# An eight-batch role adapter with layer norm: stores move to GpSimd's queue, loads are issued a batch earlier, VectorE's steps are put in another order

## The chip, the cores and the metric

The kernel runs on one core of one Trainium2 chip. The metric is the device time of one execution in microseconds. TensorE does the matrix products, VectorE and ScalarE work on the elements, GpSimd computes one small quantity per tile of rows, and SyncE issues the loads (and, before the change, the stores).

## The reference

For each of 8 batches `x` is 512 rows of 1024 columns, and a role (1 or 2, drawn per batch) picks the weights.

```python
h = einsum('bsh,bhk->bsk', x, W_down[role]) + b_down[role]     # 1024 -> 512
h = gelu(h, approximate=False)
u = einsum('bsk,bkh->bsh', h, W_up[role]) + b_up[role]         # 512 -> 1024
y = x + u
yn = (y - mean(y)) * rsqrt(var(y) + 1e-05)                     # over the 1024 columns
return yn * gamma[role] + beta[role]
```

Everything is float32.

## The kernel before, in words

**Precision by three passes.** Each float32 operand is held as a rounded part (`_hi`, made by a ScalarE copy) and a rest (`_lo`, made by a VectorE subtraction, called a split below). A product is the sum of three matmuls: hi by hi, hi by lo, lo by hi. `x` and `W_down` come in four parts of 128 x 1024 per batch (`x_stage`, `wd_stage`, 512 KB each), `W_up` in four (`wu_stage`), the residual rows in four tiles of 128 x 1024 (`rows`), and there is one buffer of each. Three rows (`b_up_row`, `gamma_row`, `beta_row`) are spread to 128 partitions for each batch.

**TensorE** (L256 to L307). A batch is a down phase and an up phase of 96 matmuls each (128x512). The down phase walks parts 0 and 1 first (48 matmuls), and then makes the four column blocks kc = 0 to 3 of `down_ps` final one after the other, 12 matmuls each. The up phase makes four row tiles t = 0 to 3 in two `up_ps` buffers, 24 matmuls each; in tile 0 the six matmuls of block kc wait for `h_split` of that block (L305). Tiles 2 and 3 of `up_ps` wait until VectorE has summed tiles 0 and 1 (L295).

**ScalarE** (L376 to L396) makes `x_hi`, `wd_hi`, `wu_hi`, applies gelu to each kc (`h_full`, L346) and rounds it (`h_hi`, L348), and computes mean and sum of squares of a row tile (L353 to L356).

**VectorE** (L519 to L556) splits `wu`, `x`, `wd` and `h`, adds `b_up` to the rows when they have landed (`bias_tile`, L479), adds `up_ps` to them with a row sum (`sum_tile`, L484), centres and scales by gamma (`centre_tile`, L501, which writes into the memory of `h_full`), and finishes with 1/deviation and beta (`finish_tile`, L515). **GpSimd** makes 1/deviation of each tile (L425, L427), in order of the tiles.

**SyncE** (L187 to L212) issues all loads and stores of a batch in one fixed order, and stands at each wait until it is met. `rows` of the next batch can be loaded into tile t only when the store of tile t has landed (L177). The order of every engine's work is the order in which the code is written.

Of the kernel before, what the change touches and what calls it, by code (L numbers as in the profile page):

```python
# [5 lines left out]
P = 128  # L6
# [10 lines left out]
def bass_role_adapter_layernorm(  # L17
# [17 lines left out]
    NLOAD = 4  # L35
# [6 lines left out]
    with ExitStack() as ctx:  # L42
# [110 lines left out]
        def _(sp):  # L153
# [29 lines left out]
            def store(b, t):  # L183
                sp.wait_ge(normed, NT * b + t + 1)
                sp.dma_start(out[b, t * P:(t + 1) * P, :], rows[:, t, :]).then_inc(stored[t], 16)
# [37 lines left out]
            for i in range(KC):  # L223
                load_wu_part(first_role, i)
            steps(0)
            with sp.Fori(1, B - 1) as b:
                steps(b)
            steps(B - 1)
            for i in range(HALVES):
# [3 lines left out]
            for t in range(NT - 1):  # L233
                sp.wait_ge(stored[t], 16 * B)
            sp.wait_ge(stored[NT - 1], 16 * (B - 1))
            sp.wait_ge(last_stored, 16 * HALVES)
# [81 lines left out]
        def _(act):  # L318
# [8 lines left out]
            def round_next_part(b, i):  # L327
# [283 lines left out]
```

## Time and profile before

| | us |
|---|---|
| three runs | 377.04, 380.54, 381.19 (median 380.54) |
| profiled execution, its own time | 377.03 |
| its span, first to last instruction | 374.9 |
| TensorE busy | 355.9 (95%) |
| VectorE busy | 288.3 (77%) |
| ScalarE busy | 184.0 (49%) |
| GpSimd busy | 41.1 (11%) |
| mean granted TensorE clock | 0.994 |

The profiled execution's own time is 2.1 us over its span, and it is at the lower end of the runs shown. Busy time counts a matmul from its start to its modelled end (390 ns), though the next one starts after 227 ns, so the waits of TensorE are read from the starts of its matmuls rather than from its share of busy time.

### The profile page before, as it was taken

To read this page: it belongs to the slowest core of one execution; us is meant where nothing else is said; L and a number is where in the kernel's file an instruction comes from. 1 tells how busy PE (TensorE), PEld (TensorE's weight loads), DVE (VectorE), ACT (ScalarE), POOL (GpSimd) and SP (SyncE) were. 2 spreads that over 40 slices of the span, in tenths; PEclk is the share of its full clock that TensorE was granted. 3 is DMA by queue.
4 is the path that set the end of the run, shared out by engine and by line. 5 is a ranking of instruction groups with operands and counts; after the bars stand their busy time and mean duration, and the time that the engine had idled before them with its cause. 6 is when DMAs were issued, how large, how long until landed. Compare 5 with 4: busy or idle time off the path is not lost.

```text
span 374.9 us, 4895 instructions
## 1 busy us (share of the span) xinstructions
PE 355.9 (95%) x1548; PEld 289.0 (77%) x1548; DVE 288.3 (77%) x293; ACT 184.0 (49%) x297; POOL 41.1 (11%) x71
## 2 busy tenths in 40 slices
PE   7999899969999999999999999999999999999991
PEld 3888678848888788877888788887888878888881
DVE  2797888598875987859877788859887598793475
ACT  4793635655156643377263753546515664335132
POOL 0000120001200041001210013000120004100011
PEclk9999999999999999999999999999999999999997
DMA  7999925996189932999249972699618994391022
GB/s 210 377 408 409 386 118 180 410 368 276 64 260 409 413 142 112 324 384 405 83 147 381 372 311 112 201 382 407 242 62 267 378 412 168 140 326 40 0 112 112
DMA packets 27081, 96.58 MB, mean 258 GB/s; under 512 B 3138, under 2 KB 3138, under 8 KB 27074
## 3 DMA queue, kind: packets, MB, share of 16 engines
q1 hardware_dynamic: 26928, 96.48, 68.1%
q8 instruction: 4, 0.07, 0.1%
q10 hardware_dynamic: 146, 0.01, 0.0%
q14 instruction: 3, 0.02, 0.0%
HBM read 79.70 MB, written 16.78 MB: 257 GB/s over the span
## 4 chain that ended last, share of the span: by engine, by line
DMA 25%; DVE 22%; PE 17%; issue 14%; POOL 9%; ACT 5%; SPq 5%; ACTq 1%; DVEq 1%; POOLq 0%
DMA out<-rows 12%; PE up_ps L251 11%; DVE rows L484 8%; DMA rows<-x 8%; POOL rstd L427 6%; PE down_ps L244 6%; DMA x_stage<-xT 5%; DVE x_lo L456 4%; DVE wd_lo L461 3%; DVE rows L515 3%; DVE h_lo L472 3%; ACT squares L356 3%; POOL var_eps L425 2%; ACT neg_mean_scaled L353 1%; SPq L178 1%
## 5 line engine op out<-in xcount | busy, mean ns | idle before, releaser
L251 PE MATMUL up_ps<-wu_hi,h_hi 128*128 128x512 f32 x256 | 80.3, 392 | 9.0 <-DVE h_lo L472 7.2
L244 PE MATMUL down_ps<-x_hi,wd_hi 128*128 128x512 f32 x256 | 81.8, 390 | 1.0 <-ACT wd_hi L407 0.9
L244 PE MATMUL down_ps<-x_lo,wd_hi 128*128 128x512 f32 x256 | 81.4, 389 | 0.0
L244 PE MATMUL down_ps<-x_hi,wd_lo 128*128 128x512 f32 x256 | 81.4, 389 | 0.0
L251 PE MATMUL up_ps<-wu_lo,h_hi 128*128 128x512 f32 x256 | 79.6, 389 | 0.0
L251 PE MATMUL up_ps<-wu_hi,h_lo 128*128 128x512 f32 x256 | 79.5, 389 | 0.0
L251 PEld LDWEIGHTS up_ps<-wu_hi,h_hi 128*128 128x128 f32 x256 | 47.4, 188 | 21.9 <-issue 9.9
L479 DVE TENSOR_TENSOR rows<-rows,b_up_row 128x1024 f32<-128x1024 f32 x32 | 38.7, 1224 | 30.8 <-DMA rows<-x 30.7
L515 DVE SCALAR_TENSOR_TENSOR rows<-h_full,rstd,beta_row 128x1024 f32<-128x1024 f32 (+1 forms) x33 | 41.2, 1252 | 22.7 <-POOL rstd L427 21.4
L353 ACT ACTIVATE neg_mean_scaled<-row_sum 128x1 f32<-128x1 f32 x31 | 6.3, 203 | 106.2 <-DVE rows L484 106.2
L244 PEld LDWEIGHTS down_ps<-x_hi,wd_hi 128*128 128x128 f32 x256 | 47.8, 188 | 11.8 <-issue 1.9
L251 PEld LDWEIGHTS up_ps<-wu_lo,h_hi 128*128 128x128 f32 x256 | 48.1, 188 | 10.1
L251 PEld LDWEIGHTS up_ps<-wu_hi,h_lo 128*128 128x128 f32 x256 | 48.1, 188 | 10.1
L244 PEld LDWEIGHTS down_ps<-x_hi,wd_lo 128*128 128x128 f32 x256 | 48.1, 188 | 10.0
L244 PEld LDWEIGHTS down_ps<-x_lo,wd_hi 128*128 128x128 f32 x256 | 48.1, 188 | 9.9
L346 ACT ACTIVATE h_full<-down_ps,b_down_all 128x512 f32<-128x512 f32 x32 | 22.0, 686 | 59.0 <-PE down_ps L244 59.0
L501 DVE SCALAR_TENSOR_TENSOR h_full<-rows,neg_mean,gamma_row 128x1024 f32<-128x1024 f32 (+1 forms) x33 | 41.2, 1251 | 10.0 <-ACT neg_mean L354 9.4
L425 POOL TENSOR_TENSOR var_eps<-var,eps 128x1 f32<-128x1 f32 x31 | 10.1, 326 | 322.9 <-ACT squares L356 322.9
L456 DVE TENSOR_TENSOR x_lo<-x_stage,x_hi 128x1024 fp32r<-128x1024 f32 x32 | 39.0, 1219 | 7.3 <-ACT x_hi L405 3.9
L484 DVE SCALAR_TENSOR_TENSOR rows<-up_ps,rows 128x1024 f32<-128x1024 f32 x31 | 37.8, 1219 | 4.1 <-PE up_ps L251 4.1
L461 DVE TENSOR_TENSOR wd_lo<-wd_stage,wd_hi 128x1024 fp32r<-128x1024 f32 x32 | 39.0, 1219 | 2.0 <-ACT wd_hi L409 1.8
L467 DVE TENSOR_TENSOR wu_lo<-wu_stage,wu_hi 128x1024 fp32r<-128x1024 f32 x32 | 37.3, 1219 | 0.2
(37 smaller groups left out, 232.9 us busy)
## 6 DMA issues: line engine op xcount, KB each, us to landing
wu_stage<-W_up SPq DMA_DIRECT2D x32, 512.0 KB, 12.6
rows<-x SPq DMA_DIRECT2D x32, 512.0 KB, 7.2
x_stage<-xT SPq DMA_DIRECT2D x31, 512.0 KB, 8.2
wd_stage<-W_down SPq DMA_DIRECT2D x31, 512.0 KB, 9.1
out<-rows SPq DMA_DIRECT2D x31, 512.0 KB, 2.6
b_up_row<-b_up SPq DMA_DIRECT2D x8, 512.0 KB, 14.0
gamma_row<-gamma SPq DMA_DIRECT2D x8, 512.0 KB, 8.9
beta_row<-beta SPq DMA_DIRECT2D x8, 512.0 KB, 9.6
```

What stands on the lines that cost most here:

```text
L244: return pe.matmul(down_ps[:, kc, :], wd_part[:, n, c * K + kc * P:c * K + (kc + 1) * P], x_part[:, n, c * S:(c + 1) * S], start=start, st ...
L251: mm = pe.matmul(up_ps[:, t % 2, half], h_part[:, kc, t * P:(t + 1) * P], wu_part[:, kc, half], start=(kc == 0 and h_part is h_hi and wu_p ...
L346: act.activation(h_full[:, kc, :], down_ps[:, kc, :], ACT.Gelu, bias=bias).then_inc(h_full_ready, 1)
L425: pool.tensor_tensor(var_eps[:, t:t + 1], var[:, t:t + 1], eps[:, :], ALU.add).then_inc(var_eps_ready, 1)
L427: pool.tensor_tensor(rstd[:, t:t + 1], var_eps[:, t:t + 1], minus_half[:, :], ALU.pow).then_inc(rstd_ready, 1)
L456: dve.tensor_tensor(x_lo[:, i, :], x_stage[:, i, :], x_hi[:, i, :].bitcast(F32), ALU.subtract).then_inc(x_split, 1)
L461: dve.tensor_tensor(wd_lo[:, i, :], wd_stage[:, i, :], wd_hi[:, i, :].bitcast(F32), ALU.subtract).then_inc(wd_split, 1)
L467: dve.tensor_tensor(wu_lo[:, i, :], wu_stage[:, i, :], wu_hi[:, i, :].bitcast(F32), ALU.subtract).then_inc(wu_split, 1)
L479: dve.tensor_tensor(rows[:, t, :], rows[:, t, :], b_up_row[:, :], ALU.add).then_inc(biased, 1)
L484: dve.scalar_tensor_tensor(out=rows[:, t, :], in0=up_ps[:, t % 2, :], scalar=1.0, in1=rows[:, t, :], op0=ALU.mult, op1=ALU.add, accum_out= ...
L501: dve.scalar_tensor_tensor(out=centred[:, t % 2, half], in0=rows[:, t, half], scalar=neg_mean[:, t:t + 1], in1=gamma_row[:, half], op0=ALU ...
L515: dve.scalar_tensor_tensor(out=rows[:, t, half], in0=centred[:, t % 2, half], scalar=rstd[:, t:t + 1], in1=beta_row[:, half], op0=ALU.mult ...
```

## The change

The first seven batches are stored by GpSimd: after the 1/deviation of each tile it waits for that tile's `finish_tile` and issues the store from its own queue. Only the last batch is still stored by SyncE. SyncE now issues the loads of `x` and `W_down` of batch b+2 at the end of its steps for batch b, where it issued those of b+1 during batch b. VectorE puts the split of `wu` parts between the steps of the last tile of the batch before, splits part 0 of `x` and `wd` ahead of the first `h`, puts one split of the next batch's part 1 between two `h` splits, and adds the bias to tile 3 behind `h` block 2; parts 2 and 3 are split before and during tile 0's steps. ScalarE makes `x_hi` of parts 0 and 1 ahead of the first gelu, and parts 2 and 3 ahead of the first variance. TensorE's program is the same.

```diff
-            def load_next_part(b, next_role, i):
-                sp.wait_ge(x_split, NLOAD * b + i + 1)
-                load_x_part(b + 1, i)
-                sp.wait_ge(wd_split, NLOAD * b + i + 1)
-                load_wd_part(next_role, i)
+            def load_ahead(batch, role, i):
+                sp.wait_ge(x_split, NLOAD * (batch - 1) + i + 1)
+                load_x_part(batch, i)
+                sp.wait_ge(wd_split, NLOAD * (batch - 1) + i + 1)
+                load_wd_part(role, i)
...
             def steps(b):
                 first, last = is_first(b), is_last(b)
                 role = load_role(sp, b)
-                if not last:
-                    next_role = load_role(sp, b + 1)
-                    load_next_part(b, next_role, 0)
-                if first:
-                    load_role_row(b_up_row, b_up, role, b_up_landed)
                 load_rows(b, 0)
                 load_rows(b, 1)
                 if not first:
-                    store(b - 1, NT - 1)
-                load_rows(b, 2)
+                    load_rows(b, 2)
+                    sp.wait_ge(normed, NT * b)
                 load_role_row(gamma_row, gamma, role, gamma_landed)
                 load_role_row(beta_row, beta, role, beta_landed)
+                if first:
+                    load_rows(b, 2)
                 load_rows(b, 3)
-                if not last:
+                if last:
+                    return
+                next_role = load_role(sp, b + 1)
+                if first:
                     for i in range(1, NLOAD):
-                        load_next_part(b, next_role, i)
-                    for i in range(KC):
-                        sp.wait_ge(wu_split, KC * b + i + 1)
-                        load_wu_part(next_role, i)
-                    sp.wait_ge(biased, NT * (b + 1))
-                    load_role_row(b_up_row, b_up, next_role, b_up_landed)
-                for t in range(NT - 1):
-                    store(b, t)
+                        load_ahead(1, next_role, i)
+                for i in range(KC):
+                    sp.wait_ge(wu_split, KC * b + i + 1)
+                    load_wu_part(next_role, i)
+                sp.wait_ge(biased, NT * (b + 1))
+                load_role_row(b_up_row, b_up, next_role, b_up_landed)
+                if isinstance(b, int) and b + 2 == B:
+                    return
+                role_after = load_role(sp, b + 2)
+                for i in range(NLOAD):
+                    load_ahead(b + 2, role_after, i)
...
@@ ScalarE
+                act.wait_ge(up_ready, NT * b)
+                round_wu(b, 0)
+                variance(b - 1, NT - 1)
+                for i in range(1, KC):
+                    round_wu(b, i)
+                if not last:
+                    round_next_part(b, 0)
+                    round_next_x(b, 1)
                 gelu(b, 0, role)
                 if not last:
-                    round_next_part(b, 0)
+                    round_wd_part(b + 1, 1)
                 gelu(b, 1, role)
                 gelu(b, 2, role)
                 gelu(b, 3, role)
                 if not last:
-                    round_next_part(b, 1)
                     round_next_part(b, 2)
+                    round_next_part(b, 3)
                 variance(b, 0)
-                if not last:
-                    round_next_part(b, 3)
...
@@ GpSimd
+            def store(b, t):
+                pool.wait_ge(normed, NT * b + t + 1)
+                pool.dma_start(out[b, t * P:(t + 1) * P, :], rows[:, t, :]).then_inc(stored[t], 16)
...
             with pool.Fori(0, B - 1) as b:
                 for t in range(NT):
                     inverse_deviation(b, t)
+                    store(b, t)
...
@@ VectorE, the first batch
+            def first_steps():
...
+                for t in range(NT):
+                    bias_tile(0, t)
+                sum_tile(0, 0)
+                split_x_part(1, 1)
+                split_wd_part(1, 1)
+                centre_tile(0, 0)
+                finish_tile(0, 0)
+                split_x_part(1, 2)
+                sum_tile(0, 1)
...
@@ VectorE, the others
+            def down_steps(b):
+                last = is_last(b)
+                sum_tile(b - 1, NT - 1)
+                split_wu(b, 0)
+                centre_tile(b - 1, NT - 1)
+                split_wu(b, 1)
+                finish_tile(b - 1, NT - 1)
+                split_wu(b, 2)
+                split_wu(b, 3)
+                for t in range(NT - 1):
+                    bias_tile(b, t)
...
+            def steps(b):
+                down_steps(b)
+                split_x_part(b + 1, 2)
+                split_wd_part(b + 1, 2)
+                sum_tile(b, 0)
+                split_x_part(b + 1, 3)
+                centre_tile(b, 0)
+                split_wd_part(b + 1, 3)
+                finish_tile(b, 0)
+                for t in range(1, NT - 1):
+                    sum_tile(b, t)
+                    centre_tile(b, t)
+                    finish_tile(b, t)
```

The first place is VectorE in the loop over the batches, around the up phase's start: before, from the four bias tiles (L479) to the end of the `h` splits (L472).

```order
L479 TENSOR_TENSOR rows<-rows,b_up_row 128x1024 [waits rows_landed0,b_up_landed]
L479 TENSOR_TENSOR rows<-rows,b_up_row 128x1024 [waits rows_landed1]
L479 TENSOR_TENSOR rows<-rows,b_up_row 128x1024 [waits rows_landed2]
L479 TENSOR_TENSOR rows<-rows,b_up_row 128x1024 [waits rows_landed3]
L472 TENSOR_TENSOR h_lo<-h_full,h_hi 128x512 [waits h_hi_ready]
L455 ISA
L456 TENSOR_TENSOR x_lo<-x_stage,x_hi 128x1024 [waits x_hi_ready]
L461 TENSOR_TENSOR wd_lo<-wd_stage,wd_hi 128x1024 [waits wd_hi_ready]
L472 TENSOR_TENSOR h_lo<-h_full,h_hi 128x512 [waits h_hi_ready] x3
```

The same place in the changed kernel, from the third bias tile on, where L512 is the bias, L490 and L495 are the splits of `x` and `wd`, and L505 is that of `h`:

```order
L512 TENSOR_TENSOR rows<-rows,b_up_row 128x1024 [waits rows_landed2]
L489 ISA
L490 TENSOR_TENSOR x_lo<-x_stage,x_hi 128x1024 [waits x_hi_ready]
L495 TENSOR_TENSOR wd_lo<-wd_stage,wd_hi 128x1024 [waits wd_hi_ready]
L505 TENSOR_TENSOR h_lo<-h_full,h_hi 128x512 [waits h_hi_ready]
L489 REGISTER_ALU
L490 TENSOR_TENSOR x_lo<-x_stage,x_hi 128x1024 [waits x_hi_ready]
L505 TENSOR_TENSOR h_lo<-h_full,h_hi 128x512 [waits h_hi_ready]
L495 TENSOR_TENSOR wd_lo<-wd_stage,wd_hi 128x1024 [waits wd_hi_ready]
L505 TENSOR_TENSOR h_lo<-h_full,h_hi 128x512 [waits h_hi_ready]
L512 TENSOR_TENSOR rows<-rows,b_up_row 128x1024 [waits rows_landed3]
L505 TENSOR_TENSOR h_lo<-h_full,h_hi 128x512 [waits h_hi_ready]
```

Between `h` blocks 0 and 1 stood an `x` and a `wd` split; now one `x` split stands there, part 0 comes ahead of all `h` splits, and the bias of tile 3, which waits for the last rows to land, has moved from ahead of block 0 to behind block 2.

The second place is GpSimd's loop, of which one tile is shown; before:

```order
L425 TENSOR_TENSOR var_eps<-var,eps 128x1 [waits var_ready]
L427 TENSOR_TENSOR rstd<-var_eps,minus_half 128x1 [waits var_eps_ready]
L424 REGISTER_ALU
L425 TENSOR_TENSOR var_eps<-var,eps 128x1 [waits var_ready]
L427 TENSOR_TENSOR rstd<-var_eps,minus_half 128x1 [waits var_eps_ready]
```

and now, with the wait for `finish_tile` (L473) and the store between two tiles' 1/deviation:

```order
L454 TENSOR_TENSOR var_eps<-var,eps 128x1 [waits var_ready]
L456 TENSOR_TENSOR rstd<-var_eps,minus_half 128x1 [waits var_eps_ready]
L473 ISA [waits normed]
L473 DMA out<-rows 128x1024
L453 REGISTER_ALU
L454 TENSOR_TENSOR var_eps<-var,eps 128x1 [waits var_ready]
L456 TENSOR_TENSOR rstd<-var_eps,minus_half 128x1 [waits var_eps_ready]
```

The third is SyncE at the start of a batch in the loop. Before, the store of tile 3 (L185) and all waits on `stored` share its queue:

```order
L161 ISA [waits x_split]
L161 DMA x_stage<-xT 128x1024
L164 ISA [waits wd_split]
L164 DMA wd_stage<-W_down 128x1024
L177 REGISTER_ALU
L178 ISA [waits stored0]
L178 DMA rows<-x 128x1024
L178 ISA [waits stored1]
L178 DMA rows<-x 128x1024
L184 ISA
L185 ISA [waits normed]
L185 DMA out<-rows 128x1024
```

and now:

```order
L179 ISA [waits stored0]
L179 DMA rows<-x 128x1024
L179 ISA [waits stored1]
L179 DMA rows<-x 128x1024
L179 ISA [waits stored2]
L179 DMA rows<-x 128x1024
L182 ISA [waits normed]
L182 DMA gamma_row<-gamma 128x1024
L182 DMA beta_row<-beta 128x1024
L179 ISA [waits stored3]
L179 DMA rows<-x 128x1024
```

The four stores are gone from SyncE, and the loads of `x` and `W_down` that stood at its start are issued at the end of the steps of two batches earlier.

## Rows read from the trace of the kernel before

**Rows 1.** The page: the span, and each engine's busy time (share, instructions)

```profile
span 374.9 us, 4895 instructions
...
PE 355.9 (95%) x1548; PEld 289.0 (77%) x1548; DVE 288.3 (77%) x293; ACT 184.0 (49%) x297; POOL 41.1 (11%) x71
```

**Rows 2.** TensorE's waits: waiting line, releaser, us in total, times, longest

```profile
PE up_ps L251 <- DVE h_lo L472: 7.2, 7, 2.2
PE up_ps L251 <- DVE rows L484: 1.8, 2, 1.6
```

**Rows 3.** Chain of waits, in order of time: start, us, what

```profile
107.17 7.77 DMA out<-rows
115.09 4.91 DMA rows<-x
...
345.35 21.77 PE up_ps L251 x96
```

**Rows 4.** TensorE's timeline, batches 0 to 2: start, duration, work, idle before

```profile
6.84 2.41 PE L244 MATMUL down_ps<-x_hi,wd_hi 128*128 128x512 f32 x8 [0.94 <-ACT wd_hi L407]
...
39.72 0.39 PE L251 MATMUL up_ps<-wu_hi,h_lo 128*128 128x512 f32 x1
...
80.28 0.70 PE L251 MATMUL up_ps<-wu_hi,h_hi 128*128 128x512 f32 x2 [1.25 <-DVE h_lo L472]
...
123.47 0.61 PE L251 MATMUL up_ps<-wu_hi,h_lo 128*128 128x512 f32 x2
124.87 0.70 PE L251 MATMUL up_ps<-wu_hi,h_hi 128*128 128x512 f32 x2 [0.78 <-DVE h_lo L472]
```

**Rows 5.** VectorE's timeline around the up phase of batch 2

```profile
105.71 1.28 DVE L515 SCALAR_TENSOR_TENSOR rows<-h_full,rstd,beta_row 128x1024 f32<-128x1024 f32 x1 [0.85 <-POOL rstd L427]
...
120.02 1.23 DVE L479 TENSOR_TENSOR rows<-rows,b_up_row 128x1024 f32<-128x1024 f32 x1 [2.59 <-DMA rows<-x]
121.16 0.69 DVE L472 TENSOR_TENSOR h_lo<-h_full,h_hi 128x512 fp32r<-128x512 f32 x1
121.77 1.22 DVE L456 TENSOR_TENSOR x_lo<-x_stage,x_hi 128x1024 fp32r<-128x1024 f32 x1
...
124.04 1.29 DVE L472 TENSOR_TENSOR h_lo<-h_full,h_hi 128x512 fp32r<-128x512 f32 x2
```

**Rows 6.** ScalarE's timeline, the rounding of h blocks 1 to 3 of batch 2

```profile
118.56 0.62 ACT L348 CAST h_hi<-h_full 128x512 fp32r<-128x512 f32 x1
...
120.87 0.62 ACT L348 CAST h_hi<-h_full 128x512 fp32r<-128x512 f32 x1
...
123.58 0.62 ACT L348 CAST h_hi<-h_full 128x512 fp32r<-128x512 f32 x1
```

**Rows 7.** VectorE's timeline in batch 0

```profile
31.34 4.62 DVE L479 TENSOR_TENSOR rows<-rows,b_up_row 128x1024 f32<-128x1024 f32 x4
...
40.46 1.22 DVE L484 SCALAR_TENSOR_TENSOR rows<-up_ps,rows 128x1024 f32<-128x1024 f32 x1
```

**Rows 8.** GpSimd and VectorE in order of time, tile 2 of batch 1

```profile
94.36 1.42 POOL L427 TENSOR_TENSOR rstd<-var_eps,minus_half 128x1 f32<-128x1 f32 x1
...
95.86 1.28 DVE L515 SCALAR_TENSOR_TENSOR rows<-h_full,rstd,beta_row 128x1024 f32<-128x1024 f32 x1 [0.50 <-POOL rstd L427]
...
99.88 0.19 POOL L425 TENSOR_TENSOR var_eps<-var,eps 128x1 f32<-128x1 f32 x1 [4.11 <-ACT squares L356]
100.15 0.55 POOL L427 TENSOR_TENSOR rstd<-var_eps,minus_half 128x1 f32<-128x1 f32 x1
```

**Rows 9.** Issues: x_stage (count, ns min/median/max, first and last); stores (count, KB, us to landing)

```profile
L161 SPq DMA_DIRECT2D x_stage<-xT x31: 332/333/3015, 3.8 to 295.9; - x31
...
out<-rows SPq DMA_DIRECT2D x31, 512.0 KB, 2.6
```

**Rows 10.** Busy us of each engine by stretch, then PEclk, DMA share, GB/s

```profile
0.00:51.00 51.00, 46.98 (x195) 35.57 (x196) 37.64 (x36) 30.41 (x41) 3.68 (x10) 1.00 0.90 340
...
145.00:189.00 44.00, 43.35 (x192) 35.61 (x191) 35.78 (x36) 22.43 (x36) 4.94 (x8) 1.00 0.72 274
```

More of the change, by code:

```diff
@@ L181, in load_role_row, with store_last @@
                 sp.dma_start(row[:, :], param[bass.ds(role, 1), :].partition_broadcast(P)).then_inc(landed, 16)
-            def store(b, t):
+            def store_last(t):
+                b = B - 1
                 sp.wait_ge(normed, NT * b + t + 1)
-                sp.dma_start(out[b, t * P:(t + 1) * P, :], rows[:, t, :]).then_inc(stored[t], 16)
+                sp.dma_start(out[b, t * P:(t + 1) * P, :], rows[:, t, :]).then_inc(last_stored, 16)
             def steps(b):
@@ L224, in _ @@
                 load_wu_part(first_role, i)
+            load_ahead(1, load_role(sp, 1), 0)
+            load_role_row(b_up_row, b_up, first_role, b_up_landed)
             steps(0)
-            with sp.Fori(1, B - 1) as b:
+            with sp.Fori(1, B - 2) as b:
                 steps(b)
+            steps(B - 2)
             steps(B - 1)
+            for t in range(NT - 1):
+                store_last(t)
             for i in range(HALVES):
@@ L232, in _ @@
                 sp.dma_start(out[B - 1, (NT - 1) * P:NT * P, half], rows[:, NT - 1, half]).then_inc(last_stored, 16)
[L233 to L236, printed above, removed]
+            for t in range(NT):
+                sp.wait_ge(stored[t], 16 * (B - 1))
+            sp.wait_ge(last_stored, 16 * (NT - 1 + HALVES))
         @block.tensor
@@ L325, in round_wd_part, with round_next_x @@
                 act.copy(wd_hi[:, i, :], wd_stage[:, i, :]).then_inc(wd_hi_ready, 1)
-            def round_next_part(b, i):
+            def round_next_x(b, i):
                 if i < NLOAD // 2:
@@ L333, in round_next_part, with round_wu @@
                 round_x_part(b + 1, i)
+            def round_next_part(b, i):
+                round_next_x(b, i)
                 round_wd_part(b + 1, i)
-            def round_wu(b):
-                for i in range(KC):
-                    act.wait_ge(wu_landed[i], 16 * (b + 1))
-                    act.copy(wu_hi[:, i, :], wu_stage[:, i, :]).then_inc(wu_hi_ready, 1)
+            def round_wu(b, i):
+                act.wait_ge(wu_landed[i], 16 * (b + 1))
+                act.copy(wu_hi[:, i, :], wu_stage[:, i, :]).then_inc(wu_hi_ready, 1)
             def gelu(b, kc, role):
@@ L374, in last_variance @@
                                    scale=H ** -0.5, accum_out=half_var[:, i:i + 1]).then_inc(half_var_ready, 1)
+            def first_steps():
+                role = load_role(act, 0)
+                for i in range(KC):
+                    round_wu(0, i)
+                gelu(0, 0, role)
+                round_next_part(0, 0)
+                gelu(0, 1, role)
+                gelu(0, 2, role)
+                gelu(0, 3, role)
+                round_next_part(0, 1)
+                variance(0, 0)
+                round_next_part(0, 2)
+                variance(0, 1)
+                round_next_part(0, 3)
+                variance(0, 2)
             def steps(b):
-                first, last = is_first(b), is_last(b)
+                last = is_last(b)
                 role = load_role(act, b)
-                if not first:
-                    variance(b - 1, NT - 1)
-                    act.wait_ge(up_ready, NT * b)
-                round_wu(b)
+                act.wait_ge(up_ready, NT * b)
[6 more added lines that the diff above has]
+                    round_next_x(b, 1)
                 gelu(b, 0, role)
                 if not last:
-                    round_next_part(b, 0)
+                    round_wd_part(b + 1, 1)
                 gelu(b, 1, role)
@@ L414, in _ @@
             act.wait_ge(b_down_landed, 16)
-            steps(0)
+            first_steps()
             with act.Fori(1, B - 1) as b:
@@ L576, in _ @@
                 split_wd_part(0, i)
-            steps(0)
+            first_steps()
             with dve.Fori(1, B - 1) as b:
```

68 lines of the change are left out of this document (34 added, 34 removed).

## The prediction

> **What bounds the kernel now.** I read the page first, then TensorE's waits, then its timeline, then back from each wait through VectorE and the chain of waits. TensorE is busy for 95% of the span, VectorE for 77% [rows 1]. TensorE's pace is that of its last phase, undisturbed: 96 matmuls in 21.77 us, 0.2267 us each [rows 3]. There are 8 x 192 = 1536 real matmuls, which need 348.2 us at that pace. The first starts at 6.84 [rows 4], and the last phase ends at 345.35 + 21.77 = 367.1 [rows 3], so TensorE lost 367.1 - 6.8 - 348.2 = 12.1 us. The span of 374.9 is then 6.8 of start, 348.2 of matmuls, 12.1 lost and 7.8 of end. Only the 12.1 can be won by this change: the start, the end and TensorE's program stay as they are.
>
> TensorE's own waits name nine places with 9.0 us of idle time [rows 2]. A restart costs more than the idle time shown: in batch 2 the matmuls from 123.47 on should have been followed at 123.47 + 0.45 = 123.92, the next start at 124.87, 0.95 later where 0.78 of idle is shown [rows 4], and the first pair after a restart is slower by another 0.09 or so. With 0.25 for each of the nine, 11.2 us. By batch: batch 0 loses the two waits for `rows`, 1.8 + 2 x 0.25 = 2.3 [rows 2]; batch 1 the longest wait for `h_lo`, 2.2 [rows 2], and one of 1.25 [rows 4], with the restarts 4.0; the other five waits for `h_lo` are 7.2 - 3.5 = 3.7 of idle, with the restarts 5.0, or 1.0 in each of batches 2 to 6. Batch 7 waits nowhere.
>
> Where do they come from? In batch 2, tile 0's block kc = 1 is wanted at 123.9, and VectorE starts that `h` split at 124.04 because an `x` and a `wd` split (121.77 to 124.04) stand ahead of it, and these because the bias of tile 3 stood 2.59 us until its rows had landed [rows 5]. The chain of waits tells why they landed late: the store issued at 107.17 took 7.77 us behind the loads in the same queue, and the load of the next rows 4.91 after it [rows 3]. So the wait is a sum of a late store, the bias tile's place, and the two splits. In batch 0 it is another one: the bias tiles end at 31.34 + 4.62 = 36.0, but the sum of tile 0 starts at 40.46 [rows 7], behind three splits of landing loads, and TensorE wants that buffer back at 39.72 + 0.23 = 39.95 [rows 4].
>
> **The change, part by part.** TensorE's work: unchanged, 348.2 us.
>
> *Batches 2 to 6.* I walk VectorE from the start D of a down phase. In batch 2 that is 123.92 - 1.36 (six matmuls) - 21.77 = 100.8, and the last tile of batch 1 is finished at 105.71 + 1.28 = 107.0, D + 6.2 [rows 5]. The change puts two `wu` splits ahead of that end (2 x 1.14, as the two splits from 121.77 to 124.04 took [rows 5]), which partly fill the idle time there, 0.85 before the finish and some before the centring: D + 7.3. Behind it stand two `wu` splits, three biases, `x` and `wd` of part 0, `h` 0, `x` of part 1, `h` 1: eight steps of 1.14 and two of 0.61, 10.3 us, so D + 17.6 if VectorE alone decides. ScalarE's roundings of `h` 1, 2 and 3 end at 119.2, 121.5 and 124.2, D + 18.4, 20.7 and 23.4 [rows 6], and the splits of 0.6 follow: `h` 1 at D + 19.0, `wd` 1 at 20.1, `h` 2 at 21.3, the bias of tile 3 at 22.4, `h` 3 at 24.0. TensorE wants them 21.77 + 1.36 after D and then every 1.36: at 23.1, 24.5 and 25.9. Every block is there, with 1.9 us to spare at the least, and that least is ScalarE's. VectorE itself has `h` 3 done at 17.6 + 3.5 = 21.1 when it waits for nobody, so it may be late by 25.9 - 21.1 = 4.8 us. Saved: 5.0 us.
>
> Tile 3's rows: the store is issued at D + 7.3 and the bias is due at D + 21.3, 14.0 us later. A store of 7.8 and a load of 4.9, the long values of the chain [rows 3], make 12.7; with the median of 2.6 for a store [rows 9], 7.5. The bias waits in neither case, and even if it did, `h` 3 alone is behind it. The loads of `x` and `W_down` issued a batch earlier cost nothing by themselves: SyncE has 0.33 us for an issue, 3.0 where its queue was full [rows 9], and the data is asked for over 20 us later. ScalarE rounds it ahead of gelu 0; the engine has 22.4 us of work in 44 [rows 10].
>
> *Batch 1.* From the end of the biases at 36.0 [rows 7] to the end of tile 3's finish VectorE now has four sums, centrings and finishes (1.2 each), six splits of `x` and `wd` and two of `wu` (1.14 each): 23.5 us, and some 1.9 of waits for mean and 1/deviation, as 0.50 in one tile [rows 8] and 0.85 in another [rows 5]. That is 61.4, and with the same ten steps `h` 1 is at 71.7, `h` 2 at 73.4, `h` 3 at 75.2. TensorE starts batch 1 at 6.84 + 0.4 (its first eight matmuls take 2.41 us [rows 4], where the pace gives 2.0) + 43.5 + 0.6 = 51.4, is through the down phase at 73.1, and wants the blocks at 74.5, 75.9 and 77.2. All hold, by 2.0 us. The last rows are there at 61.4 + 2.6 + 4.9 = 68.9, or with the long store at 74.1, when `h` 3 is 0.7 later and still in time. Saved: 4.0.
>
> *Batch 0.* The sum of tile 0 now follows the biases at 36.0, ahead of 39.95: the first wait goes. From 36.0 to the end of the sum of tile 1 stand two sums, a centring, a finish and three splits, 8.2 us, and 1.5 of waits for mean and 1/deviation: 45.7, where TensorE wants it at 39.95 + 24 x 0.2267 = 45.4. With the restart that costs 0.6. Saved: 2.3 - 0.6 = 1.7.
>
> *The new queue.* No row shows a DMA issued by GpSimd. Call its time on GpSimd s. The nearest rows are SyncE's issues, 0.33 to 3.0 us [rows 9]. From tile to tile GpSimd has this long: finish of tile 1 at 95.86 + 1.28 = 97.1, next 1/deviation wanted at 99.88 [rows 8], 2.7 us. With s = 3.0 three tiles of a batch come 0.3 later each, 0.9 us of the 4.8. So both ends cost nothing; I take 1 us, nearer to the usual issue. GpSimd's own two steps already stretch beside VectorE: 1.42 against 0.55 for the same power [rows 8], and that is in my walk. SyncE's four stores go from a queue that will wait less.
>
> A rule of the Trainium skill bears on s. "SBUF — State Buffer", section "SBUF: two separate sides", calls it the "DVE blocks DMA" trap: a DMA from GpSimd's queue has its descriptors written by that engine, and it took 3.1 us where 0.62 is usual beside a VectorE copy. The page's section "Who interferes with whom" excepts two-input operations, and these are the ones here. With 3.1 the sum stays the same; the rule raises my chance of the slower case from 0.02 to 0.05. "DMA: Bandwidth & Descriptors", section "Issuing engines are not separate DMA queues", speaks against the change too: the queues of all engines share the same DMA engines, and another queue saves only time of issue. By it a store would still take its 7.8 us, which the walk above bears; it is the reason for a third of the first rival's chance.
>
> *Sum:* 5.0 + 4.0 + 1.7 = 10.7, less 0.2 for what I may have counted twice at restarts: 10.5. From the profiled execution's 377.03 that is 366.5. The runs shown are 377.04, 380.54 and 381.19, so the profiled one is the low end and the median 3.5 above it. Runs of the changed kernel will lie from 366.5 to about 370; I take 1.5 above the low end, 368.0.
>
> **The rivals.**
>
> *The first two batches keep their waits* (0.12). For: the DMA engines are 90% busy up to 51 us [rows 10], and the change puts eight loads of batch 2, 4 MB or 10 us at 400 GB/s, ahead of batch 1's rows; the margin in batch 1 is 2.0 us. Against: they are asked for from 36 to 53, before the first of these rows can be stored and loaded. The 4.0 and 1.7 stay lost: 368.0 + 5.7 = 373.7.
>
> *The orders change and the waits stay* (0.06): the prefetch and the earlier rows would then not shorten VectorE's path to `h` 1, because ScalarE's `h`, now behind three roundings, comes late instead. Against it: `h` 1 was rounded at 119.2, and VectorE took it at 124.04 [rows 5, 6]. Then only batch 0 gains: 368.0 + 9.0 = 377.0, within 1% of the median before.
>
> *GpSimd holds up the tiles* (0.05, slower). Each store keeps GpSimd from the next tile's 1/deviation, for which VectorE stands at its finish. Three tiles of a batch are delayed by s - 2.7 each; TensorE notices from 3 x (s - 2.7) > 4.8, s = 4.3, and all the gain is used up when it loses 1.5 in each of seven batches, at s = 4.8. At s = 5.2 it loses 2.7 in each and 0.6 in batch 0, 19.5 us against 11.2: 377.0 + 8.3, with the same 1.5 for the place among the runs 386.8. For: the row of 1.42 against 0.55 shows that the two engines get in each other's way. Against: the stretch is 0.9 us and a store would have to be held over four VectorE operations.
>
> **The numbers.** The forecast has 0.77, the rivals 0.12, 0.06 and 0.05. The range of 364.5 to 374 holds the forecast, with no wait at all (another 0.6) and 1.4 for a run below the profiled one as its lower end, and the first rival as its upper. About 1% (3.8 us) is what a measurement can tell. Faster than 376.7: 0.77 + 0.12, less a little, 0.88; same 0.07; slower 0.05.
>
> **What would show it.** In the profile of the changed kernel the waits of TensorE for `h_lo` should be gone, one of some 0.3 us for the sum of a tile should be left in batch 0, and the batches should follow each other at 43.5 us (192 x 0.227), where they now take one more. The bias should no longer wait for rows, and GpSimd's stores should take under 2.7 us from one to the next step. The forecast is wrong if GpSimd's stores take over 4.3 us, if the last rows of batch 1 land after 75, or if TensorE's pace is not 0.227.

## The result, and the profile after

| | before | changed |
|---|---|---|
| median of four runs each, us | 378.79 (376.21 to 381.19) | 366.75 (365.60 to 367.49) |
| profiled execution, its own time, us | 377.03 | 366.64 |
| its span, us | 374.9 | 364.9 |

The ratio is 0.968, with a 95% interval from 0.960 to 0.976: faster by 3.2%. The three runs of before that stood ahead of the prediction had a median of 380.54. From profile to profile the span is 10.0 us shorter.

The page of the changed kernel, beside [rows 1] and [rows 9]: busy times, the queue of GpSimd's stores (packets, MB, share of the DMA engines), and the loads of `rows` and the stores (KB, us to landing).

```profile
span 364.9 us, 4944 instructions
PE 353.7 (97%) x1548; PEld 289.4 (79%) x1548; DVE 287.7 (79%) x293; ACT 185.4 (51%) x297; POOL 57.4 (16%) x99
q0 software_dynamic: 4032, 14.68, 10.3%
rows<-x SPq DMA_DIRECT2D x32, 512.0 KB, 3.4
out<-rows POOLq DMA_DIRECT2D x28, 512.0 KB, 4.8
```

No engine has less to do. VectorE's busy time is the same within 0.6 us, GpSimd has 16 us more for its 28 stores, and a store takes longer to land in the median, 4.8 against 2.6 [rows 9]. What went is waiting.

The chain of waits of the changed kernel, in order of time (start, us, what), answers [rows 3]:

```profile
29.88 21.76 PE up_ps L260 x96
51.64 21.76 PE down_ps L253 x96
73.40 2.81 PE up_ps L260 x12
76.22 0.12 issue
76.34 1.62 PE up_ps L260 x6
77.96 0.12 issue
78.08 17.93 PE up_ps L260 x78
96.00 21.76 PE down_ps L253 x96
117.76 21.76 PE up_ps L260 x96
...
335.36 21.77 PE up_ps L260 x96
```

Almost the whole chain is now TensorE: phase follows phase after 21.76 us, and a batch takes 2 x 21.76 = 43.5. Neither store nor load stands between two of its pieces any more. Its last phase ends at 335.36 + 21.77 = 357.1; with the start at 6.84 and 348.2 of matmuls it has lost 357.1 - 6.8 - 348.2 = 2.1 us, where it had lost 12.1. Of the 2.1, 1.1 is lost at the start (the second `W_down` load lands late), and some 0.8 in batch 1, seen above as two pieces of 0.12 and what a restart adds; the other seven batches lose nothing. The rest of 0.2 is no loss: the end of the last matmul is a modelled one, 0.16 later than the next start would be. For the same reason the chain dates a phase 0.16 later than its first matmul, which for batch 2's down phase is 95.84.

VectorE's timeline of the changed kernel (start, duration, work, idle before it) at three places: the end of batch 0's biases, against [rows 7], the up phase's start in batch 1, and the same in batch 2, against [rows 5]:

```profile
32.00 4.63 DVE L512 TENSOR_TENSOR rows<-rows,b_up_row 128x1024 f32<-128x1024 f32 x4
36.54 1.22 DVE L517 SCALAR_TENSOR_TENSOR rows<-up_ps,rows 128x1024 f32<-128x1024 f32 x1
...
44.19 1.22 DVE L517 SCALAR_TENSOR_TENSOR rows<-up_ps,rows 128x1024 f32<-128x1024 f32 x1
...
68.62 1.23 DVE L512 TENSOR_TENSOR rows<-rows,b_up_row 128x1024 f32<-128x1024 f32 x1 [2.14 <-DMA rows<-x]
...
75.51 0.68 DVE L505 TENSOR_TENSOR h_lo<-h_full,h_hi 128x512 fp32r<-128x512 f32 x1
...
101.40 1.27 DVE L548 SCALAR_TENSOR_TENSOR rows<-h_full,rstd,beta_row 128x1024 f32<-128x1024 f32 x1
102.59 2.35 DVE L500 TENSOR_TENSOR wu_lo<-wu_stage,wu_hi 128x1024 fp32r<-128x1024 f32 x2
...
113.84 0.69 DVE L505 TENSOR_TENSOR h_lo<-h_full,h_hi 128x512 fp32r<-128x512 f32 x1 [0.89 <-ACT h_hi L359]
...
117.16 1.22 DVE L512 TENSOR_TENSOR rows<-rows,b_up_row 128x1024 f32<-128x1024 f32 x1
119.27 0.69 DVE L505 TENSOR_TENSOR h_lo<-h_full,h_hi 128x512 fp32r<-128x512 f32 x1 [0.89 <-ACT h_hi L359]
```

In batch 2 `h` block 1 is split at 113.84, ten us before its place in [rows 5]. Five of the ten are there because the batch itself starts earlier; counted from the start of its down phase (95.84 here, 100.80 before) the split comes at 18.0 where it came at 23.2. The bias of tile 3 (117.16) waits for nothing; and block 3 is done at 119.96, where TensorE, whose up phase began at 117.60, wants it at 117.60 + 3 x 1.36 = 121.7. VectorE now waits for ScalarE's `h`, which is the sign that the row loads are out of its way.

VectorE's and GpSimd's waits of the changed kernel (waiting line, releaser, us in total, times, longest):

```profile
POOL out L473 <- DVE rows L548: 61.7, 28, 2.6
DVE h_lo L505 <- ACT h_hi L359: 27.9, 26, 3.1
DVE rows L548 <- POOL rstd L456: 17.3, 22, 0.9
DVE rows L512 <- DMA rows<-x: 2.1, 1, 2.1
```

The bias waits for rows once, in batch 1, where it had waited 30.7 us in all before. The last two fences on this kernel are GpSimd's timeline at the store of batch 1's tile 3, and the DMA issues in the stretch from 100 to 118 us:

```profile
103.32 0.59 POOL L473 DMA_DIRECT2D out<-rows  x1 [2.55 <-DVE rows L548]
```

```profile
out<-rows POOLq DMA_DIRECT2D x1, 512.0 KB, 7.8
```

The store costs GpSimd 0.59 us. It takes 7.8 us to land, as the one of [rows 3] did from SyncE's queue (7.77).

### The profile page after: what moved, and what is told of

Read it like the earlier page. It is cut to its first block, busy times and chain, and to the rows that moved or that the text cites. A ratio compares the mean times of both kernels' runs of the same rounds, so it can differ in the third digit from the quotient of the medians.

```text
span 364.9 us, 4944 instructions
## 1 busy us (share of the span) xinstructions
PE 353.7 (97%) x1548; PEld 289.4 (79%) x1548; DVE 287.7 (79%) x293; ACT 185.4 (51%) x297; POOL 57.4 (16%) x99
## 4 chain that ended last, share of the span: by engine, by line
PE 95%; DMA 2%; DVE 0%; ACT 0%; issue 0%; SPq 0%; POOL 0%; DVEq 0%; ACTq 0%; POOLq 0%
PE up_ps L260 48%; PE down_ps L253 48%; DMA wd_stage<-W_down 1%; DMA roles_sb<-roles 0%; DVE rows L548 0%; POOL half_var L462 0%; DVE rows L525 0%; SPq L140 0%; DVEq L42 0%; ACT wd_hi L438 0%; ACTq L42 0%; POOLq L42 0%; SPq L223 0%; ACT neg_mean_scaled L377 0%; POOL var_eps L465 0%
## 5 line engine op out<-in xcount | busy, mean ns | idle before, releaser
L454 POOL TENSOR_TENSOR var_eps<-var,eps 128x1 f32<-128x1 f32 x31 | 15.2, 491 | 234.7 <-ACT squares L367 234.7
L490 DVE TENSOR_TENSOR x_lo<-x_stage,x_hi 128x1024 fp32r<-128x1024 f32 x32 | 39.1, 1221 | 7.1 <-ACT x_hi L434 3.9
L505 DVE TENSOR_TENSOR h_lo<-h_full,h_hi 128x512 fp32r<-128x512 f32 x32 | 22.1, 692 | 27.9 <-ACT h_hi L359 27.9
L330 ACT CAST x_hi<-x_stage 128x1024 fp32r<-128x1024 f32 x31 | 32.5, 1048 | 21.8 <-PE down_ps L253 15.8
L495 DVE TENSOR_TENSOR wd_lo<-wd_stage,wd_hi 128x1024 fp32r<-128x1024 f32 x32 | 39.0, 1218 | 2.4 <-ACT wd_hi L438 2.2
```

The costliest lines, as they stand in the source:

```text
L330: act.copy(x_hi[:, i, :], x_stage[:, i, :]).then_inc(x_hi_ready, 1)
L454: pool.tensor_tensor(var_eps[:, t:t + 1], var[:, t:t + 1], eps[:, :], ALU.add).then_inc(var_eps_ready, 1)
L490: dve.tensor_tensor(x_lo[:, i, :], x_stage[:, i, :], x_hi[:, i, :].bitcast(F32), ALU.subtract).then_inc(x_split, 1)
L495: dve.tensor_tensor(wd_lo[:, i, :], wd_stage[:, i, :], wd_hi[:, i, :].bitcast(F32), ALU.subtract).then_inc(wd_split, 1)
L505: dve.tensor_tensor(h_lo[:, kc, :], h_full[:, kc, :], h_hi[:, kc, :].bitcast(F32), ALU.subtract).then_inc(h_split, 1)
```

## The experiments

The theory: the gain is VectorE's order, above all the bias of tile 3 behind `h` block 2, because then only `h` block 3, the last that TensorE needs, stands behind a late row tile. The first rival: the stores' own queue gets the rows in earlier, and the order matters little. The second: the loads issued a batch ahead are what pays. Each run has its own runs of the kernel before on the same chip; all times are medians in us.

**1. The stores alone.** The kernel before, with GpSimd issuing the first seven batches' stores:

```diff
-                if not first:
-                    store(b - 1, NT - 1)
                 load_rows(b, 2)
+                if not first:
+                    sp.wait_ge(normed, NT * b)
...
-                for t in range(NT - 1):
-                    store(b, t)
@@ GpSimd
                     inverse_deviation(b, t)
+                    store(b, t)
```

> The kernel before with one part of the change: GpSimd issues the stores of the first seven batches, SyncE keeps its order of loads, VectorE and ScalarE keep theirs. Theory A (the wait of 1.0 us in each of batches 2 to 6 exists because the store of tile 3 takes 7.8 us behind the loads and so the bias of tile 3 holds up h block 1): the store of tile 3 takes about 4.8 us, as in the changed kernel, the bias ends at D + 17 (D: start of the down phase), and the two splits and h 1 end at D + 21, wanted at D + 23.1. TensorE's waits in batches 2 to 6 go (-5.0), batch 1 keeps some 1.5 of 4.0, batch 0 keeps its 2.3: 7 to 8 us less than before. Rival B (the x and wd splits between h blocks 0 and 1 make the wait whenever the rows come): batches 2 to 6 keep 1.0 each, and at most 2.5 us are saved. Rival C (the queue does nothing, since all queues share the same DMA engines): store to landing stays near 8 us, same time as before.

Measured: 375.31 against 378.43, ratio 0.990 (0.984 to 0.997). TensorE's timeline of this kernel in batch 1, and below it the busy times of three stretches (the number ahead of the DMA share is the granted clock):

```profile
77.93 0.70 PE L251 MATMUL up_ps<-wu_hi,h_hi 128*128 128x512 f32 x2 [2.24 <-DVE h_lo L477]
...
80.80 1.19 PE L251 MATMUL up_ps<-wu_hi,h_hi 128*128 128x512 f32 x2 [0.69 <-DVE h_lo L477]
...
82.65 1.05 PE L251 MATMUL up_ps<-wu_hi,h_lo 128*128 128x512 f32 x2
83.50 1.05 PE L251 MATMUL up_ps<-wu_hi,h_hi 128*128 128x512 f32 x2
...
87.23 0.62 PE L251 MATMUL up_ps<-wu_hi,h_hi 128*128 128x512 f32 x2
```

```profile
78.00:81.00 3.00, 2.31 (x7) 1.39 (x8) 3.00 (x4) 1.87 (x2) 0.00 (x0) 0.63 0.99 348
81.00:84.00 3.00, 3.00 (x8) 2.32 (x9) 3.00 (x4) 2.32 (x3) 0.00 (x0) 0.50 1.03 421
84.00:87.00 3.00, 3.00 (x11) 2.38 (x10) 1.27 (x2) 0.00 (x0) 0.00 (x0) 0.73 1.03 416
```

The expectation had 7 to 8 us less; 3.1 came. The waits of batches 0 and 1 stay. In batches 2 to 6 they shrink from 5.0 to some 0.7 in all. Not because the store lands after the 4.8 us that I had expected: in batch 2 it was issued at 110.46 and the load behind it at 117.86, 7.4 us later, where 7.9 lay between them before [rows 3]. The load then landed in at most 3.7 (117.86 to the bias at 121.60) instead of 4.9, so from tile 3's finish to its bias it is 13.1 us (108.52 to 121.60) where it was 14.3 (105.71 to 120.02) [rows 5], and the five waits of about a microsecond lay just inside that difference. In batch 1, after the wait of 2.24 us, TensorE ran at half the clock for nearly seven us and lost 2.9 more than the waits of that batch explain, over half of what the other batches had gained; the span is 373.6.

**2. The bias alone.** The kernel before, with one step moved:

```diff
-                    for t in range(NT):
+                    for t in range(NT - 1):
                         bias_tile(b, t)
                 split_h(b, 0)
...
-                for kc in range(1, KC):
+                for kc in range(1, KC - 1):
                     split_h(b, kc)
+                if not first:
+                    bias_tile(b, NT - 1)
+                split_h(b, KC - 1)
```

> The kernel before with one instruction moved: VectorE adds the bias to tile 3 behind h block 2 and not ahead of h block 0 (batches 1 to 7). Stores, loads and everything else stay. Theory A: the late rows are still as late (the bias still waits 0 to 2 us for them), but only h block 3 stands behind them, which is wanted 2.7 us later than block 1; all waits for h_lo in batches 2 to 6 go (-5.0) and nearly all of batch 1's 4.0; batch 0 keeps 2.3. 8 to 9 us less than before, without any other part of the change. Rival B (the two splits between blocks 0 and 1): the wait in batches 2 to 6 shrinks by less than half, 2 to 4 us less than before. Rival D (what was won is the earlier loads): nothing here.

Measured: 367.60 against 378.43, ratio 0.973 (0.969 to 0.977). VectorE's timeline of this kernel in batch 2:

```profile
114.56 1.23 DVE L479 TENSOR_TENSOR rows<-rows,b_up_row 128x1024 f32<-128x1024 f32 x1 [1.24 <-DMA rows<-x]
115.70 0.68 DVE L472 TENSOR_TENSOR h_lo<-h_full,h_hi 128x512 fp32r<-128x512 f32 x1
...
118.58 1.29 DVE L472 TENSOR_TENSOR h_lo<-h_full,h_hi 128x512 fp32r<-128x512 f32 x2
119.78 1.22 DVE L479 TENSOR_TENSOR rows<-rows,b_up_row 128x1024 f32<-128x1024 f32 x1
```

`h` block 1 comes at 118.58 instead of 124.04 [rows 5]. Most of that is the batch's own earlier start: counted from its down phase (96.09 here, 100.80 before) it is 22.5 instead of 23.2, and those 0.7 us are the time that TensorE had lost there. The bias of tile 3 meets rows that have landed. One moved step gives 10.8 of the 12 us, and the two splits between `h` blocks 0 and 1, the other suspect, still stand where they stood. TensorE keeps 0.3 in each of batches 1 and 2 and 1.4 in batch 0.

**3. The new orders without the new queues.** SyncE and GpSimd as before, VectorE and ScalarE as in the changed kernel. The edit gives ScalarE, for one, this:

```diff
-                gelu(b, 0, role)
                 if not last:
                     round_next_part(b, 0)
+                    round_next_x(b, 1)
+                gelu(b, 0, role)
```

> The kernel before with the new orders of VectorE and ScalarE, but with SyncE's and GpSimd's programs of before: stores on SyncE's queue, x and W_down of the next batch loaded during the batch. ScalarE now rounds x part 1 ahead of the first gelu, and that part is asked for only after the load of rows tile 3 (at D + 15) and lands 8 us later, at D + 23. So all four gelus come behind it, h 3 is ready at about D + 31 where TensorE wants it at D + 25.9. Theory A (the new orders need the earlier loads): TensorE waits some 5 to 6 us in each of batches 1 to 6, 25 to 35 us more than before, near 405. Rival B (the orders carry the gain by themselves): as fast as the changed kernel, 10 us less than before.

Measured: 394.93 against 378.43, ratio 1.044 (1.040 to 1.048). ScalarE's wait for the loads of `x` in this kernel, among all waits:

```profile
ACT x_hi L321 <- DMA x_stage<-xT: 76.1, 16, 10.9
```

and its timeline in batch 2:

```profile
123.45 1.05 ACT L321 CAST x_hi<-x_stage 128x1024 fp32r<-128x1024 f32 x1 [10.89 <-DMA x_stage<-xT]
124.41 0.68 ACT L348 ACTIVATE h_full<-down_ps,b_down_all 128x512 f32<-128x512 f32 x1
```

The gelu stands behind the rounding of part 1 of `x`, whose load SyncE issued too late. The direction was expected and the size was not: 25 to 35 us more were forecast (near 405), 16.5 came, because after batch 1 TensorE lost 3 to 4 us in a batch and not 5 to 6. So ScalarE's new order needs the loads a batch ahead. Whether these loads gain anything beside that this run doesn't show, and no run has them alone; run 6 comes near it, with a kernel that is as fast without them. The moved bias can be taken out of the change by itself, ScalarE's order can't.

**4. The stores back in SyncE's queue**, all else as changed:

```diff
                 if not first:
+                    store(b - 1, NT - 1)
                     load_rows(b, 2)
-                    sp.wait_ge(normed, NT * b)
...
+                for t in range(NT - 1):
+                    store(b, t)
@@ GpSimd
                     inverse_deviation(b, t)
-                    store(b, t)
```

> The changed kernel with the stores back on SyncE's queue (tiles 0 to 2 at the end of a batch's steps, tile 3 after the loads of rows 0 and 1, as before); loads a batch ahead and both new orders stay. Theory A (GpSimd's queue is one of several sufficient cures): tile 3 finished at D + 6.7, a store of up to 7.8 and a load of 4.9 make D + 19.4, the bias is due at D + 21.2, nothing waits: the time of the changed kernel within 1 us (366 to 368). Rival C (the own queue is what the gain hangs on): the waits for h_lo come back, 4 to 9 us more than the changed kernel.

Measured: 367.17 against 378.43, ratio 0.972 (0.967 to 0.977); its profile shows 1.8 us lost in batch 1 and nothing in the others. With VectorE's order in place the new queue is worth at most that difference to the 0.8 of the changed kernel, and in the medians (the changed kernel has 366.75 and, run again, 366.56) it can't be told from nothing.

**5. The old order of the `h` block back**, all else as changed:

```diff
-                for t in range(NT - 1):
+                for t in range(NT):
                     bias_tile(b, t)
+                split_h(b, 0)
                 if not last:
                     split_x_part(b + 1, 0)
                     split_wd_part(b + 1, 0)
-                split_h(b, 0)
+                for kc in range(1, KC):
+                    split_h(b, kc)
                 if not last:
                     split_x_part(b + 1, 1)
-                split_h(b, 1)
-                if not last:
                     split_wd_part(b + 1, 1)
-                split_h(b, 2)
-                bias_tile(b, NT - 1)
-                split_h(b, 3)
```

> The changed kernel with one part undone: VectorE's order around the h blocks is that of before (bias of all four tiles ahead of h 0, x and wd of part 0 between h 0 and h 1, part 1 behind h 3). GpSimd's stores, the loads a batch earlier and ScalarE's new order stay. In the changed kernel's trace the store of tile 3 takes 7.8 us also from GpSimd's queue, and the rows are there at D + 18.7 only. Theory A (order is the cure, not the queue): bias 3 ends at D + 19.8, the two splits and h 1 at D + 23.3 to 23.5, wanted at D + 23.1: 0.3 to 0.7 us lost in each of batches 2 to 6 with the restart, and 2 to 3.5 in batch 1 where the rows come later: 4 to 6 us more than after_again. Rival B (own queue and earlier loads suffice): nothing in batches 2 to 6 and under 1 us more in all.

Measured: 375.88 against 379.55, ratio 0.992 (0.989 to 0.996), and 9.3 above the changed kernel on the same chip (366.56, last row of the table below). VectorE's timeline of this kernel in batch 2:

```profile
117.72 1.23 DVE L512 TENSOR_TENSOR rows<-rows,b_up_row 128x1024 f32<-128x1024 f32 x1 [5.44 <-DMA rows<-x]
118.86 0.69 DVE L505 TENSOR_TENSOR h_lo<-h_full,h_hi 128x512 fp32r<-128x512 f32 x1
119.46 1.22 DVE L490 TENSOR_TENSOR x_lo<-x_stage,x_hi 128x1024 fp32r<-128x1024 f32 x1
120.60 1.22 DVE L495 TENSOR_TENSOR wd_lo<-wd_stage,wd_hi 128x1024 fp32r<-128x1024 f32 x1
121.73 1.89 DVE L505 TENSOR_TENSOR h_lo<-h_full,h_hi 128x512 fp32r<-128x512 f32 x3
```

With GpSimd's queue, the loads ahead and every other new order, the bias in its old place waits 5.4 us, more than before, and the `h` blocks with it; TensorE loses 0.6 in this batch and 11.2 in the whole profile, where the changed kernel had lost 2.0. The edit puts back more than the bias: the splits of parts 0 and 1 of `x` and `W_down` return to their places too. So this run shows that the gain hangs on the order around the `h` blocks, and run 2 shows which step of it: alone it gives 10.8, and without this order 9.3 of it is gone.

**6. The fewest moves.** From run 2 on: batch 0's sum of tile 0 right behind the biases (run "minimal"); then the bias of tile 2 between `h` blocks 1 and 2 too, on the kernel before ("two on before") and on the changed one ("two on changed"):

```diff
-                for t in range(NT - 1):
+                for t in range(NT - 2):
                     bias_tile(b, t)
...
+                bias_tile(b, NT - 2)
                 split_h(b, 2)
```

What was expected of minimal:

> The kernel before with two moves on VectorE and nothing else: the bias of tile 3 behind h block 2 in batches 1 to 7, and in batch 0 the sum of tile 0 right behind the biases. Stores stay on SyncE, loads come during the batch, ScalarE's order stays. Theory A (VectorE's order carries the whole gain): bias_moved took 367.6 and lost 0.9 of it at batch 0's first sum and 0.5 at its second; the first goes: 366.7, within 0.5 us of after_again. Rival E (the other parts of the change hold a gain of their own that shows once the waits are gone): 1 us or more slower than after_again.

Of two on before:

> The kernel before with three moves on VectorE and nothing else: those of minimal (bias of tile 3 behind h 2; in batch 0 the sum of tile 0 behind the biases), and the bias of tile 2 between h 1 and h 2. minimal's profile still shows two waits of 0.18 for h 1 (0.4 each with the restart) in batches 1 and 2, since the bias of tile 2 waits 1.3 us for its rows ahead of h 0. These go: 0.9 less than minimal's 367.5, 366.6; and within 1 us of two_biases (365.6), which has everything else of the change too. If it is 1.5 us or more above two_biases, the earlier loads or the own queue are worth something once the waits are gone.

Of two on changed:

> The changed kernel with the bias of tile 2 also moved, behind the split of wd part 1 and ahead of h block 2. In batch 1 the changed kernel's VectorE waits 2.1 us for the rows of tile 2 and h blocks 2 and 3 come late, 0.75 us lost. With the bias moved h blocks 0 and 1 no longer stand behind those rows; the sum of VectorE's steps to h 2 is the same, but the 2.1 us are filled with the splits of x and wd. Expected: batch 1 loses under 0.2, 366.1 us or 0.6 less than after_again, which 5 rounds may just show. If the loss in batch 1 stays, the rows weren't its cause.

And of the changed kernel again, beside them:

> The changed kernel once more, beside the others of this call on the same chip: about 366.8 us, as measured (365.6 to 367.5). It is the yardstick for the next three.

| | median, us | lowest to highest | before, same chip | ratio (95%) |
|---|---|---|---|---|
| minimal | 367.48 | 366.42 to 368.05 | 379.55 | 0.968 (0.964 to 0.972) |
| two on before | 366.62 | 366.25 to 367.12 | 378.65 | 0.967 (0.964 to 0.971) |
| two on changed | 365.58 | 365.15 to 369.98 | 379.55 | 0.964 (0.960 to 0.969) |
| changed, again | 366.56 | 366.31 to 367.97 | 379.55 | 0.967 (0.963 to 0.971) |

Minimal missed its forecast, to be within 0.5 of the changed kernel, with 0.9: its profile lost 1.6 at the start and 0.4 and 0.5 in batches 1 and 2. The other two came in as forecast, within 0.6.

Two on before touches only VectorE's order, has SyncE's and GpSimd's programs of before, and is as fast as the changed kernel. Its page:

```profile
span 364.3 us, 4895 instructions
PE 354.3 (97%) x1548; PEld 289.8 (80%) x1548; DVE 289.0 (79%) x293; ACT 185.0 (51%) x297; POOL 41.9 (12%) x71
```

Two on changed is the fastest kernel of the study, by 1.0 us in the median, with intervals that overlap. In its profile no wait of TensorE is left after the start, while the changed kernel loses 0.8 in batch 1. Its highest run is the profiled one, where the first `W_down` loads landed late and TensorE lost some 4.7 us in its first 18, part of it at a granted clock of 0.50.

**7. How much GpSimd may be held.** The changed kernel with a fill of 128 x 2048 elements on GpSimd after each store:

```diff
                     store(b, t)
+                    pool.memset(filler[:, :], 0.0)
```

> The changed kernel with a useless fill of a 128x2048 float32 buffer on GpSimd behind each store, so that GpSimd is held for s = 0.6 + m from the finish of a tile, m to be read from the trace (the output isn't touched). Theory: VectorE comes later by s - 2.6 for three tiles of a batch, since ScalarE's sums are there 2.65 us after a finish; TensorE waits only when that sums to more than 4.8 in a batch. If m is 2 us or less, the time is that of the changed kernel (366.6, within 1). If m is 3.5, 3 x 1.5 = 4.5 and it is just still the same; if m is 5, 3 x 3.0 - 4.8 = 4.2 us more in each of seven batches, 396. Rival: a fill disturbs VectorE itself, whose steps on two operands would get longer than 1.22 us.

Measured: 367.07 against 378.65, ratio 0.968 (0.963 to 0.973). GpSimd's timeline of this kernel in batch 1:

```profile
99.28 0.59 POOL L474 DMA_DIRECT2D out<-rows  x1 [2.02 <-DVE rows L550]
99.87 1.84 POOL L483 MEMSET filler<- 128x2048 f32 x1
101.64 0.51 POOL L455 TENSOR_TENSOR var_eps<-var,eps 128x1 f32<-128x1 f32 x1
```

GpSimd is held for 0.59 + 1.84 = 2.4 us per store instead of 0.6, the longest wait of VectorE's finish grows from 0.9 to 1.2, its steps keep their 1.22, and TensorE waits nowhere in the loop (it lost 3.6 us at the start of this profile). The loss that I had put at s = 4.3 us and above was not reached; a longer hold wasn't tried, so the point from which it costs stays an estimate.

## Why the prediction was right, step by step

**The sum.** Forecast 368.0, measured 366.75; for the profiled execution 366.5 was worked out and 366.64 measured. That these two agree within 0.2 is in part luck: by the spans the terms below came to 9.9 and not 10.5, with errors of 0.8 (batch 1) and 0.6 (the start) one way and 0.6 (batch 0) the other, and 0.4 more was saved outside the span. The 1.5 between 366.5 and 368.0 was my place of the run among the others: the profiled run of before lay 3.5 below its median, and I let the changed kernel's do the same in part. Its four runs lie within 1.9 us, and the profiled one at their median. Before, runs spread over 5 us; with the waits went most of that spread.

**Batches 2 to 6** (5.0 saved): right, all of it, and by the walk. From D = 95.84 the finish of tile 3 ends at D + 6.8 (7.3 said), the bias of tile 3 at D + 22.5 (22.4), `h` 3 at D + 24.1 (24.0), 1.7 us before its need (1.9). The store takes 7.8 us, the load from 111.22 was in before 117.16. It is ScalarE that VectorE waits for, some 0.9 before blocks 1, 2 and 3.

**Batch 1** (4.0): 3.2. Here the step failed that looked at tile 3's rows alone. Tile 2's store was issued at 56.5, its load some 7 us later, and its bias, which still stands ahead of all `h` blocks, waited 2.14 for it until 68.6. The walk then ran 2 us late, its spare of 2.0 was gone, and block 2 ended at 76.19, where the matmuls for it could have started at 76.05. Two on changed takes exactly this wait away. It is the first rival in small: the early loads do crowd the DMA engines, which are 97% busy up to 51 us where they were 90% [rows 10], and from 51 to 62 us too, where they had been at 0.31. The first two lines are of the changed kernel, the third is of the kernel before:

```profile
0.00:51.00 51.00, 47.79 (x202) 37.17 (x203) 38.18 (x37) 30.30 (x41) 4.62 (x11) 1.00 0.97 368
51.00:62.00 11.00, 11.00 (x50) 9.10 (x49) 10.07 (x12) 7.46 (x13) 3.87 (x6) 1.00 1.02 414
51.00:62.00 11.00, 11.00 (x50) 9.13 (x49) 8.07 (x10) 4.54 (x10) 1.95 (x5) 1.00 0.31 112
```

In that stretch the store of batch 0's tile 2 took 6.9 us to land, where it had taken 2.6. It is the loads and not the queue: it took 6.8 in run 4, with the early loads and SyncE's queue, and 4.3 in run 1, with GpSimd's queue and without them.

**Batch 0** (1.7): 2.3. Only one of the two waits was to go, with 0.6 left for the sum of tile 1. That sum ended at 45.4, 0.3 ahead of the walk, since VectorE waited 0.6 for 1/deviation and not at all for the mean where I had 1.5; and TensorE, 0.65 later from the start on, wanted it at 46.0 only. With a start like before's there would have been little room (the second profile of the changed kernel, 0.24 late at that point, lost nothing there either): it is in part the same time counted at the start.

**The start** was held constant and lost 0.6 more. I put that down to the run and not to the change: SyncE issues the first loads in the same order in both, and the second profile of the changed kernel lost 0.1 there. It isn't shown, though: the start costs 0.5 to 1.6 us in the six profiles with SyncE's loads in the order of before, and 0.1 to 4.7 in the six with the changed one. So 2.3 + 3.2 + 5.0 - 0.6 = 9.9, and the spans say 10.0.

**The queue of the stores.** I took 1 us on GpSimd between bounds of 0.33 and 3.0; it is 0.59. The rule on the "DVE blocks DMA" trap, from "SBUF — State Buffer" of the Trainium skill, would have had 3.1; VectorE was at a two-input split when the 0.59 was taken (102.59 to 104.94), which is the case that its section "Who interferes with whom" excepts, and the trace agrees with the exception. The other rule, from "DMA: Bandwidth & Descriptors", section "Issuing engines are not separate DMA queues", was the better guide: 7.8 us from GpSimd's queue, 7.8 from SyncE's. Run 4 says the same in time.

**The rivals.** That the waits stay because ScalarE comes late: refuted, though run 3 shows where it would have come true, without the loads ahead, at 394.9. That GpSimd holds the tiles: not at 0.6, nor at 2.4 us.

**What I had right for the wrong share.** I put the gain down to rows, order and queue together. Run 2 puts nine tenths of it down to one step's place, run 5 agrees, and run 6 puts all of it down to VectorE alone. Batches 2 to 6 had two cures, each nearly enough by itself: 1.2 us less from finish to bias (run 1), or a bias that only the last `h` block waits behind (run 2). The expectation for run 5 missed the same thing: the old place was to cost 4 to 6 and cost 9.3. Batch 2 lost 0.6, as forecast, but batch 1 lost 4.2 where the changed kernel loses 0.8, and batches 3 and 4 lost 2.1 and 2.4. There the rows of tile 3 are asked for later in the batch: in batch 3 the store of the last tile was issued 8.2 us after the start of the down phase, where it had been 6.4 before, it took 8.6 to land, and the load behind it was issued at 17.0 instead of 14.2. The bias waits 43 us in all, not 31.

## What to carry to other kernels

A step that waits for a late transfer should be issued as late as its own consumer allows, and behind the steps that the bound engine waits for; look at what stands behind it in its queue before moving the transfer. Another queue for a transfer saves its place in the order, not the time that it takes to land. When an engine's order is changed so that it needs data earlier, look for the load that has to move with it: alone, such an order may cost more than the whole change brings.

## What the runs showed of the hardware

TensorE's granted clock fell to 0.50 (1.2 of 2.4 GHz) after some waits in mid-kernel: pairs of matmuls then followed each other after 0.85 us instead of 0.45 for 3 to 7 us. It did so after waits of 2.24, 2.25, 2.48 and 5.72 us (runs 1 and 3), and each time TensorE lost 1.7 to 2.9 us beyond the waits. It didn't fall after one of 2.23 in the kernel before, one of 2.44 in run 5, or any of 2.1 and less in mid-kernel. In the first 18 us it also fell in three profiles, around idle times of 2.31 (minimal) and of 1.7 (two on changed, run 7). So a wait costs more than it shows in some cases; what decides in which the runs don't tell.

Beside it, a fill of 128 x 2048 float32 elements took GpSimd 1.84 us, and didn't stretch VectorE's steps beside it.
